# Moving the rounding of the first convolution's input from VectorE to GpSimd, in a block of three convolutions

## What is computed

```
x = x + conv0(gn(x))
x = x + conv12(gn(x))

gn(v):      group norm, 16 groups of 2 channels, per image
conv0(v):   s = max|v| over all images;  q = round(v * 127 / s)
            3x3 convolution of q with weights quantised in the same way,
            times s*sw/127^2, plus bias
conv12(v):  h = lrelu(instance_norm(conv3x3(v, kern1)))
            return lrelu(instance_norm(conv3x3(h, kern2)))
            kern = einsum(weight, fixed basis), slope 0.2
```

## Time and profile before

| | us |
|---|---|
| median of 3 runs | 409.96 |
| lowest and highest of them | 408.22, 411.0 |
| the profiled execution's own time | 408.46 |
| its span, first to last instruction | 406.7 |
| busy: PE / DVE / ACT / POOL | 311.2 / 304.6 / 230.4 / 106.7 |
| mean granted clock of PE | 0.976 of full speed |

### The profile page before, as it was taken

How to read it: one execution, slowest core, us unless ns; L and a number is a source line. 1 busy time by engine, 2 the same in 40 slices (tenths; PEclk the granted TensorE clock), 3 DMA queues, 4 the chain that set the end, 5 groups by cost and what they waited for, 6 DMA issues and landing times.

```text
span 406.7 us, 11776 instructions
## 1 busy us (share of the span) xinstructions
PE 311.2 (77%) x5344; PEld 127.9 (31%) x5344; DVE 304.6 (75%) x446; ACT 230.4 (57%) x239; POOL 106.7 (26%) x184
## 2 busy tenths in 40 slices
PE   0000100658999999999999999999999999997970
PEld 0000100526343334334333433333343334333520
DVE  3829899694487789769887977897697889557144
ACT  1089995444162774485476618645853775285434
POOL 0289867106030303302130313033020400100000
PEclk9999999997999999999999999999999999998995
DMA  7999400000000031005001300400050022005005
GB/s 268 406 421 432 171 1 1 2 0 2 3 2 3 2 156 56 2 3 208 2 3 79 132 2 2 180 32 2 3 208 3 2 105 106 2 3 209 2 2 206
DMA packets 4178, 34.79 MB, mean 86 GB/s; under 512 B 608, under 2 KB 768, under 8 KB 1280
## 3 DMA queue, kind: packets, MB, share of 16 engines
q1 hardware_dynamic: 4128, 34.04, 20.5%
HBM read 17.26 MB, written 16.78 MB: 84 GB/s over the span
## 4 chain that ended last, share of the span: by engine, by line
PE 52%; DVE 36%; POOL 4%; issue 2%; DMA 2%; ACT 1%; SPq 0%; DVEq 0%; POOLq 0%
PE ring L818 36%; DVE bn_c L688 10%; PE ring L870 8%; DVE amax L620 7%; DVE xs L705 7%; DVE qpad L665 4%; PE ring L824 3%; DMA xs<-w_dram 2%; PE ring L777 2%; POOL apad L485 2%; PE gathered_in L770 2%; DVE own_stat_c L695 1%; DVE bn_x L678 1%; DVE xs L672 1%; DVE bn_x L598 1%
## 5 line engine op out<-in xcount | busy, mean ns | idle before, releaser
L688 DVE BATCH_NORM_STATS2 bn_c<-ring 128x6 f32<-128x512 f32 x128 | 82.6, 687 | 59.6 <-PE ring L824 59.6
L338 ACT COPY apad<-ring 128x1024 f32<-128x1024 f32 x32 | 32.2, 1006 | 62.6 <-DVE bn_c L688 62.6
L818 PE MATMUL ring<-hpad,own 64*32 64x512 f32 x512 | 67.1, 592 | 0.0
L824 PE MATMUL ring<-apad,own 64*32 64x512 f32 x512 | 67.1, 592 | 0.0
L818 PE MATMUL ring<-apad,own 64*32 64x512 f32 x512 | 66.9, 592 | 0.0
L824 PE MATMUL ring<-hpad,own 64*32 64x512 f32 x512 | 66.9, 592 | 0.0
L824 PE MATMUL ring<-apad,side 64*32 64x512 f32 x512 | 66.6, 587 | 0.0
L818 PE MATMUL ring<-hpad,vert 64*32 64x512 f32 x512 | 66.6, 587 | 0.0
L818 PE MATMUL ring<-apad,vert 64*32 64x512 f32 x512 | 66.4, 587 | 0.0
L824 PE MATMUL ring<-hpad,side 64*32 64x512 f32 x512 | 66.3, 587 | 0.0
L338 ACT COPY hpad<-ring 128x1024 f32<-128x1024 f32 x32 | 32.5, 1016 | 35.0 <-DVE bn_c L688 34.4
(11 more groups left out here) (109 smaller groups left out, 476.5 us busy)
## 6 DMA issues: line engine op xcount, KB each, us to landing
xs<-x_dram SPq DMA_DIRECT2D x8, 2048.0 KB, 9.8
out_dram<-xs SPq DMA_DIRECT2D x14, 1024.0 KB, 3.9
out_dram<-xs SPq DMA_DIRECT2D x4, 512.0 KB, 2.9
xs<-w_dram SPq DMA_DIRECT2D x1, 288.0 KB, 9.8
const<-const_dram SPq DMA_DIRECT2D x1, 146.0 KB, 2.4
xs<-w_dram SPq DMA_DIRECT2D x1, 36.0 KB, 1.6
bias<-bias_dram SPq DMA_DIRECT2D x1, 0.5 KB, 2.2
```

The lines of the kernel that those rows point to most:

```text
L338: nc.scalar.copy(unit_of(tile, u), grid(slot(FIRST[v] + u))).then_inc(taken[v], 1)
L688: ins = nc.vector.bn_stats(bn[s][:, u * UBANKS + h, :], ring[:, (FIRST[v] + u) % SLOTS, h, :])
L818: nc.tensor.matmul(bank_out(u, v, hp, C * (2 * px + py), C), wv[q0:q0 + 64, v - 1, px, py, :], window(tile, u * UBANKS + hp, dy, 0, q0, 64 ...
L824: ins = nc.tensor.matmul(bank_out(u, v, hx, C * (2 * px + py), C), ws[q0:q0 + 64, v - 1, px, py, :], window(tile, u * UBANKS + hx, 0, dx, ...
```

## The change

From image 1 on, POOL does all of the quantisation. `affine` keeps its first pass into `scaled`, adds a second in place that adds `ROUND`, and a third that subtracts `ROUND` and writes float16 rows into `qpad`. A new semaphore `q_step_pool` orders the three passes of a piece. The wait for conv0 of the image before, which stood ahead of DVE's first piece, stands now ahead of the third pass of POOL's first piece. DVE's four calls of `rounded` leave its period; its rounding of image 0 stays. The order of the pieces among POOL's other work stays as it was.

```diff
 def affine(b, n):
     r0, r1 = EDGES[n:n + 2]
+    rows = scaled[n % 2][:, 0:(r1 - r0) * BLK]
+    at = 4 * (b - 1) + n
     pool.wait_ge(q_ready, 4 * b + max(n - 1, 0))
-    nc.gpsimd.tensor_scalar(scaled[n % 2][:, 0:(r1 - r0) * BLK], xs_rows(b, r0, r1), q_scale[:, b:b + 1],
-                            q_shift[:, b:b + 1], ALU.mult, ALU.add).then_inc(q_scaled, 1)
+    nc.gpsimd.tensor_scalar(rows, xs_rows(b, r0, r1), q_scale[:, b:b + 1], q_shift[:, b:b + 1],
+                            ALU.mult, ALU.add).then_inc(q_step_pool, 1)
+    pool.wait_ge(q_step_pool, 2 * at + 1)
+    nc.gpsimd.tensor_scalar(rows, rows, 1.0, ROUND, ALU.mult, ALU.add).then_inc(q_step_pool, 1)
+    if n == 0:
+        pool.wait_ge(conv_done[0], UNITS * b)
+    pool.wait_ge(q_step_pool, 2 * at + 2)
+    nc.gpsimd.tensor_scalar(rows_of(qpad, r0, r1), grid(rows), 1.0, -ROUND, ALU.mult, ALU.add
+                            ).then_inc(q_ready, 1)
...
 def rounded(b, n):
     r0, r1 = EDGES[n:n + 2]
-    if n == 0 and b > 0:
-        dve.wait_ge(conv_done[0], UNITS * b)
     dve.wait_ge(q_scaled, 4 * b + n + 1)
...
     if after:
         group_moments("x1", t + 1)
-    if t + 2 < B:
-        rounded(t + 2, 0)
-        rounded(t + 2, 1)
     if now:
         if not after:
             conv_stats(2, t, 1)
         conv_stats(2, t, 2)
-    if t + 2 < B:
-        rounded(t + 2, 2)
-        rounded(t + 2, 3)
```

More of the change, by code:

```diff
@@ L198, in conv_block_kernel @@
         q_ready = sem("q_ready")
+        q_step_pool = sem("q_step_pool")
         a_ready = sem("a_ready")
```

## The result

| | before | changed |
|---|---|---|
| median, us | 410.26 (4 runs, 408.22 to 411.0) | 405.5 (4 runs, 405.03 to 405.87) |
| ratio to before | | 0.9895, interval 0.9877 to 0.9914 |
| profiled execution, us | 408.46 (span 406.7) | 405.03 (span 403.1) |

A forecast was written before the change was run, and what follows sets the result against it. PE bounds the kernel behind a stall from DVE's rounding of pieces 2 and 3. 408.46 - 6 x 0.62 = 404.8 for the profiled execution, 406.3 from the median; forecast between them 405.5, range 403 to 412.

The forecast's parts named there:

- The stall and its size: Gather of conv2's moments comes late through DVE's rounding; period 37.04 against 36.42 in period 6, 0.62 us in six periods.
- the pair: DVE's two roundings of pieces 2 and 3, between statistics of conv2's units 2 and 3; 2.44 us on the chain.
- Pieces 0 and 1 lie in DVE's idle time: DVE's roundings of pieces 0 and 1 stand in idle time before unit 2, so only 0.62 a period counts.
- the 0.47 against 0.19: POOL's last norm_x1 instruction takes 0.47 us beside DVE's pair, 0.19 without; counted inside the 0.62.
- The price of a pass: Each new POOL pass taken as 1.16 us plus a 0.09 gap; upper bound 2.37 for the third pass.
- The cover: norm_c(2) on POOL 1.13 us late; slack of 1.35 at ACT and DVE before unit 1's statistics leaves 0.22.
- The lock: POOL passes hold DVE instructions with two SBUF inputs; spread_c done by +6.67, gather due +6.87: hidden, 0.2 us to spare.
- (a): Rival: slower POOL passes at pieces 2 and 3 make POOL the bound; typically 413, up to 417.9; chance 0.22.
- (b): Rival: gaps of 0.25 or passes of 1.3 eat the gain, stall moves to conv1's gather; 407.5 to 410; chance 0.17.
- (c): Rival: the stall of 0.30 before conv1's gather goes too, 6 x 0.92 = 5.5 us saved, 403.5; chance 0.06.
- the 0.30 before the gather in conv0: PE's wait inside conv0 for conv1's gather, which starts at 300.58 where matmul steps would have had it at 300.28.
- (d): Rival: image 0's path or conv0 suffers, PE waiting for q_ready; given nothing of its own.

The follow-up runs named there:

- The later set: The changed kernel measured once more, unaltered, in five rounds: 406.0, ratio 0.9908 to the kernel before.
- experiment 1: Against the kernel before: pieces 0 and 1 rounded by POOL, pieces 2 and 3 by DVE at their old place; 409.02, ratio 0.999.
- experiment 5: Changed kernel with three more POOL passes of 960 columns ahead of norm_c(2) in six periods; 426.64, ratio 1.0396 to before.
- experiment 7: Changed kernel with POOL's pieces 2 and 3 behind norm_c(2) instead of ahead of it; 409.71, ratio 0.9992 to before.
- Experiment 3: Kernel before, nothing moved to POOL; DVE rounds pieces 2 and 3 later, behind conv2's moments; 405.72, ratio 0.9894.
- experiments 8 and 6: 8: kernel before, all rounding on DVE, three moves of place; 402.75, ratio 0.9815. 6: changed kernel, DVE's last output behind conv1's spread; 402.78, ratio 0.9822.

## Why the prediction was right, point by point

- **The stall and its size.** Right. The period without rounding on DVE was read from period 6 as 36.42 and is 36.42. Six times 0.62 is 3.7, the spans differ by 3.6 (406.7 - 403.1). The forecast of 404.8 for the profiled execution met 405.03; the median forecast, 405.5, met 405.5. That it met to the tenth is luck: the number was put between 404.8 and 406.3, and the scatter outside the periods is of that size. The later set has 406.0.
- **Why the pair cost 0.62.** Incomplete. The prediction took the pair's 2.44 us on the chain as its own work. Some 0.8 of it was being held by POOL's first passes, and by the estimate in experiment 1 the pair without this hold would have been covered. The forecast did not depend on it, because it took the size from period 6.
- **"Pieces 0 and 1 lie in DVE's idle time".** Right in the full change, incomplete as a cause. DVE's own idle time covers them, but they held POOL's `norm_x1`, and through it POOL's first passes and then DVE's own pieces 2 and 3. Alone they are worth 0.27 us a period (experiment 1). The prediction saw the 0.47 against 0.19 and put it inside the 0.62, but the expectation of experiment 1 ("stays at 37.0") forgot it.
- **The price of a pass.** Mis-sized on the safe side: 1.16 was taken, the further passes took 1.05 for 1024 columns and 0.99 to 1.00 for 960. The gap was 0.08 to 0.09, as read. POOL was free at +8.16 (284.13 + 1.00 - 276.97) instead of +8.74, and its busy time rose by 56 us, not 65.
- **The cover.** 0.22 us to spare was forecast, 0.66 idle was left, and one more pass showed 0.74. The cheaper passes account for it: 8.74 - 8.24 = 0.50, and 0.22 + 0.50 = 0.72. That lateness beyond the cover costs one to one was right (experiment 5, 38.90), until PE's gap brought the clock down.
- **The lock.** `spread_c` was held for 0.51 us (0.68 against 0.17) and was still in time, as worked out. That outputs would be held if passes lasted into them was a sentence beside the sum; experiment 7 shows it and its price of 0.86 us a period.
- **Rivals.** (a) and (b) needed dearer passes and fell with the rows of the passes. (c) wanted the 0.30 before the gather in conv0 to go by itself; it did not, and needed a move of its own. (d) did not show.
- **"DVE's amount of work".** The prediction argued from place. Experiment 3 shows that the same DVE work at another place gains 0.48 of the 0.62, and experiments 8 and 6 that with the other moves it gains as much as handing it over.

## What to carry to other kernels

Ask where in its engine's order an operation stands before asking which engine should do it: 56 us of POOL's spare time bought hardly more than a move of two calls on DVE (0.14 us a period), and with the other moves nothing. If some period of the kernel lacks the suspect by itself (here the last images, which have nothing more to round), its length is the best measure of what removing it can give. When work goes to GpSimd, list the DVE instructions that will then run beside it: here those with two SBUF inputs (`spread_c`, the outputs) and the one-input roundings (L665) were held, and held POOL in turn, for up to the rest of an instruction. An instruction that looks dear where it stands may be so because it is being held: compare its time with the same instruction elsewhere.

## What was not expected of the hardware

- The GpSimd passes with immediate numbers took 1.05 us, the one whose factor and addend are columns in SBUF 1.20. The latter also reads another tile (`xs`), so the cause is not isolated. Writing float16 rows of 64 cost no more than writing float32 in place. The groups of POOL by form in the changed kernel (busy us, mean ns):

```profile
L517 POOL TENSOR_SCALAR scaled<-xs,q_scale,q_shift 128x1024 f32<-128x1024 f32 x14 | 16.8, 1198 | 0.0
L520 POOL TENSOR_SCALAR scaled<-scaled 128x1024 f32<-128x1024 f32 x14 | 14.7, 1048 | 1.2
L525 POOL TENSOR_SCALAR qpad<-scaled 128x1024 f16<-128x1024 f32 x14 | 14.7, 1048 | 1.2
```

- Being held can pass through a chain of small things: DVE's pieces 0 and 1 held a POOL instruction on one column, which delayed two POOL passes, which held DVE's pieces 2 and 3.
- A gap of 2.3 us in PE cost 1.6 us more through the clock in four periods of six; the same gap in the other two did not (experiment 5).
